# Loops written out on SyncE, TensorE and VectorE in a graph network's edge passes, and places freed eight at a time

## The chip, the cores and the metric

The kernel runs on one core of a Trainium2 chip. The core has a tensor engine (PE), a vector engine (DVE), a scalar engine (ACT), GpSimd (POOL), and SyncE (SP), which here only waits, counts and starts DMAs. Each engine works through its own program in order, and the engines meet at semaphores. The metric is the device time in microseconds (us) from the first to the last instruction; less is better.

## The reference

There are 12500 nodes with 128 features and 200000 edges, sorted by target. Two graph networks run one after the other.

```python
h = jnp.maximum(_layernorm(x, axis=-1), 0.0)
x = x + _L0_gnn_ref(h, src, dst, ...)          # two SAGE layers, each: segment_sum(h[src], dst) / degree, then a dense layer
h = jnp.maximum(_layernorm(x, axis=-1), 0.0)
x = x + _L1_gnn_ref(h, edge_index, edge_weight1, ...)   # two attention layers:
    # q, k, v = h @ Wq, h @ Wk, h @ Wv;  score = q[tgt] . (k[src] + e)
    # softmax of the scores over the edges of a target;  out = segment_sum(a * (v[src] + e), tgt)
    # gate with h @ Wskip, batch norm, relu, residual
```

## The kernel before, in words

The edges are cut into 1564 tiles of 128. A tile that crosses from one block of 128 target nodes into the next is visited once for each block, which makes 1664 steps. 32 steps are a chunk (52 chunks), two chunks are a pair (26 pairs), and 4 steps or 4 tiles are a group.

Four passes go over the edges: two aggregation passes (`sage_edges`, tags `first` and `second`) and two attention passes (`conv_edges`, one for each layer). Between them stand dense phases, and barriers part all phases.

**Aggregation pass.** POOL gathers one tile of source rows with each indirect DMA (L765) into a ring of 64 places, that is 16 groups. Before each group it waits until the semaphore `place_free` has come far enough (L761). ACT builds the one-hot matrices of the next chunk (`build`, L795 and L798) and releases the current step groups to PE one by one (`release`, L781 to L788), after it has read from small tables what tiles and PSUM banks the group needs. PE multiplies (L870), with the place and the bank of each step taken from registers that it loads from a table (L857). SP sits between PE and POOL: for each tile group it waits for the gathers (L718, which tells ACT through `tiles_in`), reads from the table `lastuse` which step group uses an older group of places last (L724 to L726), waits for that step group's sums (L727) and frees the places. The group freed is the one 8 groups back (`BEHIND`). DVE only moves finished banks out.

**Attention pass.** For each chunk DVE multiplies the gathered keys by PE's queries and sums them to scores (`multiply` L1478, `edge_term` L1493, `score_sum` L1483), runs a softmax that goes back and forth between DVE, PE and ACT (L1533 to L1586), weighs the values (L1506) and adds the 32 partial sums of PE (L1678) to the accumulators one after another (`add`, L1600 to L1606). The scores of the next chunk are worked in between. POOL gathers keys and values (L1457) and waits before each group for PE's sums of the chunk that used the places before. SP loads the small tables of the next chunk.

Chained instructions of one engine go through `Chain`: each counts a semaphore up, and `need` (L89) waits for a count. Inside a hardware loop (`Fori`, `chain.turns`) that count is a register, `self.base + mark`, so that the engine works it out first. The same holds for all waits and addresses that depend on the loop's number.

Of the kernel before, what the change touches and what calls it, by code (L numbers as in the profile page):

```python
# [41 lines left out]
KG = CH // GR  # L42
# [3 lines left out]
PAIRS = NC_ // 2  # L46
# [15 lines left out]
LAPS, REST = divmod(GROUPS, 2 * RG)  # L62
EARLY = 8
SUM_BANKS = 4
BEHIND = RG // 2
# [622 lines left out]
def sage_edges(nc, t, table, src_cols, tag, own, weight, bias):  # L688

    with room(nc, tag) as (sb, psum, sem):  # L690
# [16 lines left out]
        place_free, tiles_in, away_ready, sel_built, sel_ready, sums_ready, bank_free, chain_v = (  # L707
            sem(k) for k in ("place_free", "tiles_in", "away_ready", "sel_built", "sel_ready", "sums_ready", "bank_free", "chain_v"))

        with nc.Block() as block:  # L710
            @block.sync
            def _(sp):
# [7 lines left out]
                def half_lap(half, first):  # L720
                    for k in range(RG):
                        landed(k, half)
                        if k >= BEHIND or not first:
                            last = sp.value_load(lastuse[0:1, bass.ds(half * RG + (k - BEHIND), 1)],  # L724
                                                 min_val=0, max_val=STEPS // GR - 1)
                            sp.wait_ge(sums_ready, last + 1)  # L726
                            sp.sem_inc(place_free, 1)  # L727

# [18 lines left out]
                load_src(1, 3)  # L747
                with sp.Fori(1, LAPS - 1) as g:
                    for b in range(2):
                        half_lap(g * 2 + b, False)  # L750
                        load_src(b, g * 2 + (b + 2))
# [98 lines left out]
            def _(pe):  # L850
# [28 lines left out]
                pair(0)  # L879
                with pe.Fori(1, 2 * LAPS) as g:  # L880
                    pair(g)
# [459 lines left out]
KP = CH // PAIR  # L1341
# [8 lines left out]
def conv_edges(nc, t, tag):  # L1350

    with room(nc, tag) as (sb, psum, sem):
# [63 lines left out]
        with nc.Block() as block:  # L1416
            @block.sync
            def _(sp):
# [7 lines left out]

                with sp.Fori(0, PAIRS) as g:
                    for h in range(2):
# [33 lines left out]
            def _(dve):  # L1462
                chain = Chain(dve, chain_v)
# [172 lines left out]
                stages(chunk(0, 1), chunk(0, 0))  # L1636
                with chain.turns(PAIRS - 1, 2 * (2 * KG + 15 + KP)) as g:
                    stages(chunk(g + 1, 0), chunk(g, 1))
                    stages(chunk(g + 1, 1), chunk(g + 1, 0))
# [3 lines left out]
            def _(pe):  # L1643
# [78 lines left out]
                stages(chunk(0, 1), chunk(0, 0), chunk(1, 0))  # L1722
                with pe.Fori(0, PAIRS - 2) as g:
                    stages(chunk(g + 1, 0), chunk(g, 1), chunk(g + 1, 1))
                    stages(chunk(g + 1, 1), chunk(g + 1, 0), chunk(g + 2, 0))
# [457 lines left out]
```

## Time and profile before

| | us |
|---|---|
| median of 3 runs | 12163.2 |
| lowest, highest | 12148.79, 12170.95 |
| the profiled execution: its time | 12124.62 |
| its span, first to last instruction | 12122.7 |
| POOL busy | 6650.8 |
| PE busy | 5591.6 |
| ACT busy | 4685.4 |
| DVE busy | 3794.2 |

No engine is busy for much more than half of the span. The busy time leaves out everything that a sequencer does by itself: register work, branches, waits, DMA starts. The profile marks those with a q (SPq, DVEq), and it writes "issue" where an engine stood idle and waited for nothing that the profile shows, "remote" where the semaphore's source isn't in the record.

### The profile page before, as it was taken

The numbers are of one execution on the slowest core, as the hardware profiler recorded it, in microseconds if no ns is written. First come the engines' busy times: TensorE is split into PE (matmuls) and PEld (weight loads), VectorE is DVE, ScalarE is ACT, GpSimd is POOL, SyncE is SP. The second block draws the span as 40 slices with busy tenths as digits, with TensorE's granted clock in tenths as the row PEclk, the third lists the DMA queues.
The fourth block names the chain that finished last, engine by engine and source line by source line (L and its number), as shares of the span: only waits on it lengthen the run. The fifth ranks groups of instructions, "written<-read, shape, count | busy, mean of one in ns | idle before, by whom it ended". The sixth has DMA issues, their size and how long they took to land. (4 is left out here: it accounts for less than half of the span.)

```text
span 12122.7 us, 136052 instructions
## 1 busy us (share of the span) xinstructions
PE 5591.6 (46%) x23720; PEld 4740.3 (39%) x23721; DVE 3794.2 (31%) x11057; ACT 4685.4 (39%) x11029; POOL 6650.8 (55%) x6852
## 2 busy tenths in 40 slices
PE   0333333344443343454555555555645555555556
PEld 0333333333333333333444444444434444444444
DVE  3000000001000000034445554544744455545447
ACT  2333333333333333343444444444334444444443
POOL 4665555554565555555555555555445555555555
PEclk8555555566555555566666666666866666666667
DMA  5111111124111111134333333333243333333333
GB/s 102 50 52 49 49 50 49 49 65 128 49 51 50 48 48 49 48 104 124 113 112 112 111 113 110 111 114 113 79 131 112 111 112 109 115 111 111 113 113 88
DMA packets 623121, 1069.90 MB, mean 88 GB/s; under 512 B 213469, under 2 KB 396798, under 8 KB 622482
## 3 DMA queue, kind: packets, MB, share of 16 engines
q0 software_dynamic: 261920, 645.88, 19.2%
q1 hardware_dynamic: 281842, 368.09, 9.7%
q10 hardware_dynamic: 78848, 51.39, 1.5%
q14 instruction: 468, 3.83, 0.1%
q8 instruction: 43, 0.70, 0.0%
HBM read 961.58 MB, written 103.26 MB: 88 GB/s over the span
## 5 line engine op out<-in xcount | busy, mean ns | idle before, releaser
L1457 POOL DMA_INDIRECT conv_kv<-key_value,conv_src x3328 | 3287.0, 988 | 2925.8 <-PE conv_ps_sums L1678 1423.8
L1678 PE MATMUL conv_ps_sums<-conv_kv,conv_sel 128*128 128x136 f32 x6656 | 1509.3, 388 | 1428.2 <-DVE sums L1606 1124.7
L765 POOL DMA_INDIRECT second_msg<-sage_hidden_projected,second_src x1564 | 1477.1, 944 | 1135.3 <-SPq L727 534.2
L765 POOL DMA_INDIRECT first_msg<-sage_in,first_src x1564 | 1477.1, 944 | 1058.4 <-SPq L727 516.6
L1678 PEld LDWEIGHTS conv_ps_sums<-conv_kv,conv_sel 128*128 128x128 f32 x6656 | 1315.2, 280 | 1573.7 <-DVE sums L1606 1212.6
L1758 ACT ACTIVATE conv_selT<-conv_place,minus_partition 128x512 f32<-128x512 f32 x832 | 595.5, 716 | 3094.5 <-PE conv_ps_query L1664 1087.7
L1664 PE MATMUL conv_ps_query<-query_table,conv_selT 128*128 x6656 | 1585.8, 413 | 325.4 <-issue 277.2
L1664 PEld LDWEIGHTS conv_ps_query<-query_table,conv_selT 128*128 128x128 f32 x6656 | 1410.6, 308 | 420.6 <-issue 406.4
L870 PE MATMUL first_ps_sums<-first_msg,first_sel 128*128 x3328 | 832.0, 429 | 1524.4 <-ACTq L788 786.1
L870 PE MATMUL second_ps_sums<-second_msg,second_sel 128*128 x3328 | 832.7, 429 | 1473.6 <-ACTq L788 789.6
L1606 DVE TENSOR_TENSOR sums<-sums,conv_ps_sums 128x136 f32 x3328 | 972.5, 292 | 1506.2 <-remote 732.8
L870 PEld LDWEIGHTS first_ps_sums<-first_msg,first_sel 128*128 128x128 f32 x3328 | 718.5, 319 | 1651.1 <-issue 1651.1
L870 PEld LDWEIGHTS second_ps_sums<-second_msg,second_sel 128*128 128x128 f32 x3328 | 719.7, 319 | 1586.0 <-issue 1586.0
L1743 ACT ACTIVATE conv_sel<-iota_row,conv_rel 128x128 f32<-128x128 f32 x3328 | 1051.9, 386 | 59.7 <-PE conv_ps_sums L1678 59.1
L795 ACT ACTIVATE second_sel<-iota_row,second_rel 128x128 f32<-128x128 f32 x1664 | 556.9, 392 | 1185.0 <-issue 961.8
L795 ACT ACTIVATE first_sel<-iota_row,first_rel 128x128 f32<-128x128 f32 x1664 | 557.4, 392 | 1162.4 <-issue 922.6
L1478 DVE TENSOR_TENSOR conv_kv<-conv_ps_query,conv_kv 128x512 f32<-128x512 f32 x832 | 572.2, 688 | 1073.4 <-DMA after_hT<-conv_in_transposed 355.4
L834 DVE COPY sums<-second_ps_sums 128x129 f32 (+1 forms) x98 | 28.7, 293 | 2447.3 <-PE second_ps_sums L870 1112.0
L834 DVE COPY sums<-first_ps_sums 128x129 f32 (+1 forms) x98 | 28.7, 293 | 2426.5 <-PE first_ps_sums L870 1113.0
L1483 DVE TENSOR_REDUCE conv_score<-conv_kv 128x16 f32<-128x512 f32 x832 | 568.0, 683 | 0.0
L1763 ACT ACTIVATE conv_selT<-conv_selT 128x512 f32<-128x512 f32 x832 | 523.9, 630 | 61.9
L1746 ACT ACTIVATE conv_sel<-conv_sel 128x512 f32<-128x512 f32 x832 | 523.9, 630 | 26.3
(255 smaller groups left out, 5229.3 us busy)
## 6 DMA issues: line engine op xcount, KB each, us to landing
conv_place<-place_rows SPq DMA_DIRECT2D x416, 512.0 KB
conv_kv<-key_value,conv_src POOLq DMA_INDIRECT x3328
first_msg<-sage_in,first_src POOLq DMA_INDIRECT x1564
second_msg<-sage_hidden_projected,second_src POOLq DMA_INDIRECT x1564
conv_pen<-run_penalties SPq DMA_DIRECT2D x416, 48.5 KB
sage_own_hidden<-first_own_out ACTq DMA_DIRECT2D x49, 256.0 KB
sage_dense_own<-sage_own_hidden SPq DMA_DIRECT2D x14, 896.0 KB
sage_hidden_transposed<-sage_dense_hid SPq DMA_DIRECT2D x14, 896.0 KB
```

What stands on the lines that cost most here:

```text
L765: pool.indirect_dma_start(msg[:, j * MW:j * MW + D], None, table, bass.IndirectOffsetOnAxis(ap=src[:, b, j:j + 1], axis=0)).then_inc(gathe ...
L795: act.activation(sel[:, lo + i, :], t.iota[:, :], ACT.Abs, bias=rel[:, bass.ds(c * CH + (k * GR + i), 1)], scale=-1.0).then_inc(away_ready, 1)
L870: last = pe.matmul(ps[:, bass.ds(to[j] * 512, MW)], sel[:, h * CH + k * GR + i, :], msg[:, bass.ds(at[j] * MW, MW)], start=False, stop=Fal ...
L1457: pool.indirect_dma_start(kv[:, h * CH + j, :], None, t.kv_d, bass.IndirectOffsetOnAxis(ap=src[:, h, j:j + 1], axis=0)).then_inc(gathered[ ...
L1478: return mark(dve.tensor_tensor(keys, query(k)[:, :, :, 0:D], keys, ALU.mult))
L1483: return mark(dve.tensor_reduce(score[:, h, :, k * GR:k * GR + GR].rearrange("p h i -> p i h"), slots(h, k)[:, :, 0:D].rearrange("p i (h c ...
L1606: ins = dve.tensor_tensor(acc, acc, sums_of(h, step), ALU.add)
L1664: last = pe.matmul(psQ[:, 2 * (k % 2) + i // 2, (i % 2) * QW:(i % 2) * QW + QW], selT[:, k % SELG, P * i:P * i + P], t.qreg[:, bass.ds(at[ ...
L1678: last = pe.matmul(sums_of(h, step), sel[:, k % SELG, step % GR, :], kv[:, h * CH + step, DEN:2 * D], start=True, stop=True)
L1743: act.activation(sel[:, k % SELG, i, :], t.iota[:, :], ACT.Abs, bias=rel[:, h, j:j + 1], scale=-1.0).then_inc(away_ready, 1)
L1746: act.activation(sel[:, k % SELG, :, :], sel[:, k % SELG, :, :], ACT.Relu, bias=1.0, scale=-1.0).then_inc(sel_ready, 1)
L1758: act.activation(selT[:, k % SELG, :], place[:, q % 2, (k % 2) * GR * P:(k % 2 + 1) * GR * P], ACT.Abs, bias=t.minus[:, 0:1]).then_inc(awa ...
```

## The change

Loops that were hardware loops are now loops of the program's writer, so that each turn stands in the program with constants for its waits and addresses. This is done for SP and PE in all four edge passes, and for DVE in the two attention passes. ACT and POOL keep their loops, and so does DVE in the aggregation passes. Besides, SP frees the places of the aggregation ring for two groups at once, after the second of them.

```diff
                     for k in range(RG):
                         landed(k, half)
-                        if k >= BEHIND or not first:
+                        if k % 2 == 1 and (k >= BEHIND or not first):
                             last = sp.value_load(lastuse[0:1, bass.ds(half * RG + (k - BEHIND), 1)],
                                                  min_val=0, max_val=STEPS // GR - 1)
                             sp.wait_ge(sums_ready, last + 1)
-                            sp.sem_inc(place_free, 1)
+                            sp.sem_inc(place_free, 2)
...
-                with sp.Fori(1, LAPS - 1) as g:
+                for g in range(1, LAPS - 1):
...
-                with pe.Fori(1, 2 * LAPS) as g:
+                for g in range(1, 2 * LAPS):
...
-                with sp.Fori(0, PAIRS) as g:
+                for g in range(PAIRS):
...
-                with chain.turns(PAIRS - 1, 2 * (2 * KG + 15 + KP)) as g:
+                for g in range(PAIRS - 1):
...
-                with pe.Fori(0, PAIRS - 2) as g:
+                for g in range(PAIRS - 2):
```

```order
L1600 REGISTER_ALU
L1602 REGISTER_ALU [waits conv0_sums_ready]
L1606 ISA [waits conv0_ps_used]
L1606 TENSOR_TENSOR sums<-sums,conv_ps_sums 128x136
L89 REGISTER_ALU
L1606 ISA [waits first_gathered11]
L1606 TENSOR_TENSOR sums<-sums,conv_ps_sums 128x136
L95 REGISTER_ALU
L95 COMPARE_AND_BRANCH
L1533 TENSOR_TENSOR conv_score<-conv_score,conv_qwe 128x128 [waits first_gathered11,first_bank_free]
```

These are the same engine and place after the change.

```order
L1606 ISA [waits conv0_ps_used,conv0_sums_ready]
L1606 TENSOR_TENSOR sums<-sums,conv_ps_sums 128x136
L1606 ISA [waits first_gathered11]
L1606 TENSOR_TENSOR sums<-sums,conv_ps_sums 128x136
L1533 TENSOR_TENSOR conv_score<-conv_score,conv_qwe 128x128 [waits first_gathered11,first_bank_free]
```

Three of seven instructions of two adds are gone, and the branch with them. The address of the accumulator is still worked out (`ISA`), since it comes from a table.

The next rows are SP's in the first aggregation pass, before the change, for two tile groups.

```order
L724 ISA [waits first_sums_ready,first_gathered8]
L724 TENSOR_LOAD first_lastuse
L724 ISA x2
L726 REGISTER_ALU
L724 ISA [waits first_sums_ready,first_gathered9]
L724 TENSOR_LOAD first_lastuse
L724 ISA x2
L726 REGISTER_ALU
```

And these are SP's after the change, again for two tile groups.

```order
L724 TENSOR_LOAD first_lastuse [waits first_sums_ready,first_gathered8,first_gathered9]
L724 ISA x2
L726 REGISTER_ALU
```

One table read now serves two groups, and it comes after both have landed. On POOL nothing is moved: it asks for the places of one group at a time as before.

## Rows read from the trace of the kernel before

**Rows 1.** Stages of the program by engine; columns are in the first line.

```profile
core 0: us, PE busy (x) PEld busy (x) DVE busy (x) ACT busy (x) POOL busy (x), PEclk, DMA share, GB/s
215.00:2703.00 2488.00, 914.00 (x3625) 781.89 (x3626) 48.54 (x207) 877.72 (x2227) 1477.15 (x1564) 0.56 0.19 50
...
5500.00:8605.00 3105.00, 1588.53 (x7158) 1405.74 (x7159) 1542.89 (x4722) 1326.06 (x3017) 1641.43 (x1664) 0.63 0.37 111
```

**Rows 2.** Waits, 215 to 2703 us: who for whom, total us, times, longest.

```profile
ACT first_sel L795 <- issue: 922.6, 390, 15.0
PE first_ps_sums L870 <- ACTq L788: 786.1, 210, 26.1
POOL first_msg L765 <- SPq L727: 516.6, 142, 13.1
...
ACT first_sel L795 <- SPq L718: 74.1, 50, 6.3
```

**Rows 3.** SP's own waits in the same stretch.

```profile
SPq L727 <- PE first_ps_sums L870: 685.0, 180, 14.7
SPq L727 <- remote: 598.2, 95, 22.5
```

**Rows 4.** POOL's timeline from 1509 us: start, length, idle time before.

```profile
1511.18 0.94 POOL L765 DMA_INDIRECT first_msg<-sage_in,first_src  x1 [3.86 <-SPq L727]
1512.43 0.94 POOL L765 DMA_INDIRECT first_msg<-sage_in,first_src  x1 [0.30 <-issue]
...
1527.60 0.94 POOL L765 DMA_INDIRECT first_msg<-sage_in,first_src  x1 [1.74 <-SPq L727]
...
1540.37 0.94 POOL L765 DMA_INDIRECT first_msg<-sage_in,first_src  x1 [8.07 <-SPq L727]
...
1556.83 0.94 POOL L765 DMA_INDIRECT first_msg<-sage_in,first_src  x1 [1.77 <-SPq L727]
```

**Rows 5.** ACT's timeline around two releases, in the same columns.

```profile
1506.15 0.40 ACT L795 ACTIVATE first_sel<-iota_row,first_rel 128x128 f32<-128x128 f32 x1 [1.01 <-issue]
1507.54 0.40 ACT L795 ACTIVATE first_sel<-iota_row,first_rel 128x128 f32<-128x128 f32 x1 [0.99 <-issue]
...
1511.15 1.28 ACT L795 ACTIVATE first_sel<-iota_row,first_rel 128x128 f32<-128x128 f32 x4 [1.58 <-DVE first_ps_sums L835]
...
1514.09 1.28 ACT L795 ACTIVATE first_sel<-iota_row,first_rel 128x128 f32<-128x128 f32 x4 [1.00 <-SPq L718]
```

**Rows 6.** Register instructions of SP at L724: ns shortest/median/longest.

```profile
L724 SPq FUSED_REGOPS  x1392: 2/51/1408, 265.3 to 5279.5; - x199
```

**Rows 7.** Waits of the whole program: total us, times, longest.

```profile
POOL conv_kv L1457 <- PE conv_ps_sums L1678: 1423.8, 181, 32.3
DVE sums L1606 <- remote: 732.8, 150, 7.8
DVE sums L1606 <- issue: 398.9, 275, 5.3
DVE conv_score L1533 <- issue: 153.0, 48, 3.7
DVE sums L1606 <- PE conv_ps_sums L1678: 109.3, 94, 2.6
```

**Rows 8.** DVE's timeline over one pair of chunks in layer 1.

```profile
7071.45 0.35 DVE L1533 TENSOR_TENSOR conv_score<-conv_score,conv_qwe 128x128 f32<-128x128 f32 x1 [3.54 <-issue]
...
7117.17 0.30 DVE L1606 TENSOR_TENSOR sums<-sums,conv_ps_sums 128x136 f32 x1 [1.83 <-issue]
...
7126.97 0.28 DVE L1533 TENSOR_TENSOR conv_score<-conv_score,conv_qwe 128x128 f32<-128x128 f32 x1
...
7187.82 0.29 DVE L1533 TENSOR_TENSOR conv_score<-conv_score,conv_qwe 128x128 f32<-128x128 f32 x1 [3.08 <-issue]
```

**Rows 9.** POOL's timeline in the same pair, at two pauses.

```profile
7106.44 0.95 POOL L1457 DMA_INDIRECT conv_kv<-key_value,conv_src  x1 [3.09 <-PE conv_ps_sums L1678]
...
7124.38 0.95 POOL L1457 DMA_INDIRECT conv_kv<-key_value,conv_src  x1 [3.21 <-remote]
```

## The prediction

> **What bounds the kernel now.** I read the stages first [rows 1]. An aggregation pass takes 2488 us and an attention pass 3105; each has a twin of the same length within 1%, so the four make some 11190 of 12123 us. In neither kind is an engine busy for more than 60% of the time, so the bound is a chain of waits, and the change is in the code of exactly these stages.
>
> Then I read who waits for whom in the first aggregation pass [rows 2, 3]. A gather and the idle time behind it take 1.25 us (starts at 1511.18 and 1512.43 [rows 4]), so the 1564 gathers need 1955 us, and POOL alone isn't the bound. POOL stands 516.6 us for SP's L727 [rows 2], but SP itself stands at L727 for 685.0 + 598.2 us, 685.0 of it for PE's sums [rows 3]: SP passes on PE's lateness, it doesn't make it. PE in turn stands 786.1 us for ACT's release at L788, and ACT has 922.6 us of idle time with no releaser but its own issue [rows 2]. ACT waits only 74.1 us for SP's news of landed tiles. So the pass is held by ACT and PE, and ACT keeps its loop.
>
> What is ACT's "issue" time? Two instructions of one group start 1.39 us apart where they need 0.40 us (1506.15 and 1507.54), and soon after four of them take 1.28 us together, and two whole groups start 2.94 us apart (1511.15 and 1514.09) [rows 5]. SP's register instructions have a median of 51 ns and a longest of 1408 [rows 6]. So there are stretches in which an instruction takes some 0.7 us (half of 1.39, with one register instruction between two ACTIVATEs) instead of 0.05 on its sequencer. They lie late in POOL's unbroken runs of gathers: ACT was slow at 1506 to 1508, quick at 1511 to 1514 after POOL had paused for 3.86 us [rows 4, 5]. In the attention pass DVE's add at 7117.17 stands behind 1.83 us of "issue", late in the run of gathers that began at 7106.44 [rows 8, 9]. I call these the slow stretches. Work that becomes faster lets POOL go on without a pause, and that makes more of them; this feedback is what I expect to eat most of a gain.
>
> In the attention passes POOL stands 1423.8 us for PE's sums [rows 7], so there DVE and PE, with the chain between them, set the pace. DVE's own stalls at the adds are 398.9 us of "issue" (275 times) and 732.8 us "remote", and 153.0 us of "issue" (48 times, 3.2 us each) stand before L1533, the first instruction behind the loop's branch [rows 7].
>
> **The change part by part.** The sum is made against the profiled execution, 12124.6 us; the median of the runs, 12163.2, is 38.6 higher.
>
> SP written out in the aggregation passes: its program for two groups falls to under half. SP is waiting at L727 for half of the pass, and what waits for it in turn waits for PE. 0 us. If that cover were gone, it would be worth at most POOL's 516.6 us in this pass.
>
> PE written out there: one register instruction for a step group of 4, about 0.05 us, worked out ahead while PE waits for ACT. 0 us. The same in the attention passes, where PE waits for DVE.
>
> Places freed by eights: the first group of each pair is freed one PE group later. Nothing is queued behind POOL's wait but gathers. The cost has two ends. Low: 0, since POOL has 2488 - 1955 = 533 us to spare in a pass and fills a ring of 16 groups. High: of the four runs that [rows 4] begins, those at 1527.60 and 1556.83 are of a single group (their gathers end long before the next run). Such a run is over before a slow stretch begins; doubled, it lasts 10 us, and 5 of those may be slow. With a step group at 2.94 us when quick and about 9.7 us when slow (4 + 1 ACTIVATEs and 2 instructions of the release, times 1.39 us), 5 slow us lose 3.5 us. With at most 142 stalls in a pass [rows 2], a half of them before single groups, and half of these joined, that is 35 x 3.5 = 120 us a pass. I take 35 a pass, nearer to the low end, because POOL has its 533 us to spare, and a longer pause also gives back quick time: **+70 us** for both, bounds 0 and +240.
>
> DVE's branch: 153.0 us gross. But the pair shown tells what a pause is worth. From 7071.45 (after a pause of 3.54) to 7126.97 is 55.5 us; from 7126.97 (no pause) to 7187.82 is 60.9, of which 3.08 are the next pause, so 57.8 [rows 8]. The half without the pause before it needs 2.3 us more: two thirds of the pause are given back, as the softmax then meets a slow stretch. So a third of 153 is left: **-50 us**, bounds -153 and 0.
>
> [...]
>
> DVE's register work at the adds: 7 instructions for two adds become 4 (the listing above), and `multiply` loses two of its own. In quick stretches they run beside the previous add and cost nothing; only behind a real wait one of 0.09 us stands in the way, 94 + 150 times [rows 7]: **-20 us**. In slow stretches each counts. 3/7 of the 398.9 us of issue are 171 us. PE stands in the same slow stretch and must deliver the next sums, and POOL's pause of 3.09 or 3.21 us behind it [rows 9] shrinks by as much as DVE gains, so I take half: **-85 us**, bounds 0 and -171. If the "remote" stalls are of the same kind, 3/7 of 732.8 = 314 us more are to be had; I leave them out, since a semaphore that comes late isn't DVE's own instruction, and they extend the range.
>
> SP written out in the attention passes: it loads tables a chunk ahead, hidden behind 58 us of chunk. 0 us.
>
> Sum: +70 - 50 - 20 - 85 = -85 us, 12040 for the profiled execution, **12078** for the median.
>
> **The rivals.** (1) The forecast, a small gain: 12000 to 12135. Chance 0.38. (2) A large gain: the slow stretches become rarer because fewer instructions are issued, or the remote stalls shrink too. Then -153 - 171 - 314 = -640 at the far end, half of it 320: 11840. For it speaks that 1132 us of DVE's idle time stands before the adds; against it that ACT, with no change, has the same stalls, and that they follow POOL's runs. Chance 0.17. (3) Slower, by the eights: a run of one group becomes one of two. It decides when more than about 22 single runs in each pass are joined (22 x 3.5 x 2 = 154, against a gain of 155 at DVE). At its high end it gives +240 - 155 = +85 us or, if the gain at DVE is given back too, +240: 12250 to 12400; the likeliest is near the lower, 12270. For it: two of four runs shown are single. Against: POOL's 533 us to spare. Chance 0.29. (4) Nothing is left: the feedback takes back what DVE gains as it took two thirds of the branch's pause: 12163. Chance 0.16.
>
> **How the numbers follow.** About 0.2%, 24 us, is what a measurement of this kernel can tell from no change: the three runs lie 22 us apart. The time is that of (1), 12078. The range must hold 8 in 10: from 11840, the middle of (2), to 12280, just over the middle of (3); (1) alone is 12000 to 12135. Faster by over 0.2% are (1) but for its edge, and (2): 0.55. Same is (4) with little from (1) and (3): 0.17. Slower: 0.28.
>
> **What would show it.** In the profile after: the row "DVE conv_score L1533 <- issue" gone; attention passes some 75 us shorter each with "DVE sums L1606 <- issue" near 230; a pair's two halves alike, at 57 us or so. Aggregation passes 0 to 60 us longer, with fewer and longer stalls of POOL on SP, none shorter than a gather of eight apart, and ACT's issue time as it was. The prediction is wrong if an aggregation pass changes by over 120 us, which would mean that SP or PE was on its path, or if ACT's issue time falls, which would mean that the slow stretches depend on how many instructions the others issue. If the attention passes don't move although the branch's row is gone, the feedback is stronger than I took it.

## The result and the profile after

The changed kernel takes 11825.6 us (median of 4 runs, 11812.31 to 11838.88), the kernel before 12164.4 us beside it. The ratio is 0.9723 (95%: 0.9706 to 0.974), so the change gives 339 us. The forecast was 12078, a gain of 85, with a range from 11840; the result lies below that range. The profiled execution took 11830.03 us, its span is 11828.1, and the numbers below are from it.

These are the stages of the changed kernel that answer to [rows 1], an aggregation and an attention pass.

```profile
core 0: us, PE busy (x) PEld busy (x) DVE busy (x) ACT busy (x) POOL busy (x), PEclk, DMA share, GB/s
215.00:2728.00 2513.00, 906.44 (x3561) 774.53 (x3562) 44.76 (x197) 880.02 (x2227) 1475.33 (x1564) 0.55 0.19 50
5560.00:8492.00 2932.00, 1494.97 (x7160) 1342.26 (x7160) 1540.79 (x4722) 1320.44 (x3017) 1639.04 (x1664) 0.65 0.39 117
```

The attention pass is 173 us shorter (2932 against 3105). The next rows are DVE's adds of both attention passes, first in the kernel before and then in the changed one (ns shortest/median/longest, start of the first and of the last).

```profile
L1606 DVE TENSOR_TENSOR sums<-sums,conv_ps_sums x3328: 279/295/298, 5620.5 to 11945.8; 128x136 f32 x196
```

```profile
L1606 DVE TENSOR_TENSOR sums<-sums,conv_ps_sums x3328: 281/295/299, 5681.1 to 11653.5; 128x136 f32 x196
```

From the first to the last it is 6325 us before and 5972 after, 353 less. The first add comes 61 us later than before (5681.1 against 5620.5), so in these two executions the aggregation passes are longer by about that much. (One pair of executions says little here: in the kernel of the next section with DVE's attention loop alone, whose aggregation passes are those of before, the first add comes at 5672.9. The cost of the eights is read from the times below.) All of the gain is in the attention passes, and it is more than twice the 155 us that I forecast for them.

The waits of the whole program after the change answer to [rows 7] and, for ACT and POOL's L765, to [rows 2].

```profile
ACT first_sel L795 <- issue: 965.6, 397, 14.3
...
POOL conv_kv L1457 <- PE conv_ps_sums L1678: 908.3, 111, 32.3
...
POOL conv_kv L1457 <- remote: 627.2, 199, 3.3
...
POOL first_msg L765 <- SPq L727: 553.0, 103, 12.7
...
DVE sums L1606 <- issue: 243.2, 409, 3.8
...
DVE sums L1606 <- PE conv_ps_sums L1678: 128.1, 75, 3.1
...
DVE sums L1606 <- remote: 101.2, 64, 5.2
```

The kernel before has this row for POOL beside that of PE's sums:

```profile
POOL conv_kv L1457 <- remote: 457.4, 154, 3.4
```

The reader is to see four things. The row of L1533 behind the branch is gone. DVE's "issue" time at the adds fell from 398.9 to 243.2 us, as forecast (230). But the "remote" row, which I had left out of the sum, fell from 732.8 to 101.2: that is the largest move of all. And POOL stands 908.3 us for PE's sums where it stood 1423.8. A part of that only changed its name, since POOL's "remote" row rose from 457.4 to 627.2: the two together fell from 1881 to 1536 us, by 346, which is close to the 353 us that the attention passes gained. In aggregation ACT's issue time is as it was (922.6, now 965.6; in the three kernels of the next section that leave the aggregation passes alone it is 990.8, 942.1 and 985.6), and POOL has fewer stalls on SP that are longer (103 of 5.4 us each, before 142 of 3.6).

The timeline of DVE's L1533 after the change, one pair of chunks in the first attention pass, shows the two halves alike.

```profile
6823.36 0.28 DVE L1533 TENSOR_TENSOR conv_score<-conv_score,conv_qwe 128x128 f32<-128x128 f32 x1
...
6878.15 0.28 DVE L1533 TENSOR_TENSOR conv_score<-conv_score,conv_qwe 128x128 f32<-128x128 f32 x1
...
6934.21 0.28 DVE L1533 TENSOR_TENSOR conv_score<-conv_score,conv_qwe 128x128 f32<-128x128 f32 x1
```

That is 54.8 and 56.1 us. In [rows 8], which are from the same pass, the halves took 55.5 and 60.9.

### The profile page after: what moved, and what is told of

Same layout as the page of the kernel before. It is cut to its first block and busy times, and to the rows that moved or that the text cites. A ratio compares the mean times of both kernels' runs of the same rounds, so it can differ in the third digit from the quotient of the medians.

```text
span 11828.1 us, 120392 instructions
## 1 busy us (share of the span) xinstructions
PE 5386.2 (46%) x23720; PEld 4598.9 (39%) x23720; DVE 3790.0 (32%) x11057; ACT 4674.4 (40%) x11029; POOL 6635.3 (56%) x6852
## 5 line engine op out<-in xcount | busy, mean ns | idle before, releaser
L1457 POOL DMA_INDIRECT conv_kv<-key_value,conv_src x3328 | 3278.6, 985 | 2582.2 <-issue 927.6
L765 POOL DMA_INDIRECT second_msg<-sage_hidden_projected,second_src x1564 | 1475.2, 943 | 1160.3 <-SPq L727 548.4
L765 POOL DMA_INDIRECT first_msg<-sage_in,first_src x1564 | 1475.3, 943 | 1099.9 <-SPq L727 553.0
L1678 PE MATMUL conv_ps_sums<-conv_kv,conv_sel 128*128 128x136 f32 x6656 | 1442.3, 382 | 1096.1 <-DVE sums L1606 1018.9
L1664 PE MATMUL conv_ps_query<-query_table,conv_selT 128*128 x6656 | 1462.7, 388 | 287.9 <-issue 271.6
L1664 PEld LDWEIGHTS conv_ps_query<-query_table,conv_selT 128*128 128x128 f32 x6656 | 1296.9, 286 | 361.9 <-issue 338.3
L1606 DVE TENSOR_TENSOR sums<-sums,conv_ps_sums 128x136 f32 x3328 | 975.0, 293 | 784.9 <-issue 243.2
L1478 DVE TENSOR_TENSOR conv_kv<-conv_ps_query,conv_kv 128x512 f32<-128x512 f32 x832 | 569.4, 684 | 1663.5 <-remote 623.3
L795 ACT ACTIVATE first_sel<-iota_row,first_rel 128x128 f32<-128x128 f32 x1664 | 559.2, 392 | 1235.7 <-issue 965.6
L795 ACT ACTIVATE second_sel<-iota_row,second_rel 128x128 f32<-128x128 f32 x1664 | 556.9, 392 | 1211.2 <-issue 944.2
```

Of the source, the lines that this page charges most:

```text
L765: pool.indirect_dma_start(msg[:, j * MW:j * MW + D], None, table, bass.IndirectOffsetOnAxis(ap=src[:, b, j:j + 1], axis=0)).then_inc(gathe ...
L795: act.activation(sel[:, lo + i, :], t.iota[:, :], ACT.Abs, bias=rel[:, bass.ds(c * CH + (k * GR + i), 1)], scale=-1.0).then_inc(away_ready, 1)
L1457: pool.indirect_dma_start(kv[:, h * CH + j, :], None, t.kv_d, bass.IndirectOffsetOnAxis(ap=src[:, h, j:j + 1], axis=0)).then_inc(gathered[ ...
L1478: return mark(dve.tensor_tensor(keys, query(k)[:, :, :, 0:D], keys, ALU.mult))
L1606: ins = dve.tensor_tensor(acc, acc, sums_of(h, step), ALU.add)
L1664: last = pe.matmul(psQ[:, 2 * (k % 2) + i // 2, (i % 2) * QW:(i % 2) * QW + QW], selT[:, k % SELG, P * i:P * i + P], t.qreg[:, bass.ds(at[ ...
```

## The experiments

Runs on two groups of chips come up here, and they must be kept apart. On one group the kernel before takes 12164 to 12173 us; the profile shown ahead of the prediction, the result and the first eight experiments are from such chips. On the other group it takes 9099 to 9109 us. I call them the 12.2 ms chips and the 9.1 ms chips. The experiments on the first group are from two chips, those on the second from three. Each chip was used in one set of runs only, and the first group's came earlier, so the runs can't tell a property of the chip from a condition of the time. Each ratio is to the kernel before on the same chip.

**One part at a time, in the kernel before.** Four kernels, each the kernel before with one edit: DVE's attention loop, PE's, SP's, and the places by eights, in the order of this diff.

```diff
-                with chain.turns(PAIRS - 1, 2 * (2 * KG + 15 + KP)) as g:
+                for g in range(PAIRS - 1):
...
-                with pe.Fori(0, PAIRS - 2) as g:
+                for g in range(PAIRS - 2):
...
-                with sp.Fori(0, PAIRS) as g:
+                for g in range(PAIRS):
...
-                        if k >= BEHIND or not first:
+                        if k % 2 == 1 and (k >= BEHIND or not first):
...
-                            sp.sem_inc(place_free, 1)
+                            sp.sem_inc(place_free, 2)
```

Expected, DVE's attention loop:

> The kernel before with one edit: DVE's attention loop written out. In the changed kernel a chunk of the attention passes takes 55.0 us instead of 58.4, 3.4 x 104 = 355 us in all, and the aggregation passes are 57 us longer. Theory A (DVE's instructions were the cost: the branch comes back in full and its register work at the adds too, 'remote' stalls included): this kernel alone has nearly the whole of the 355, ratio 0.970 to 0.975, the 'remote' idle time of DVE at the adds falls from 733 us to under 200. Theory B (my forecast, the gain of DVE is half given back): ratio 0.987 to 0.992. Theory C (SP or PE written out in the attention passes carries a good part): ratio 0.980 to 0.990 with the remote stalls still above 400 us.

Expected, PE's attention loop:

> The kernel before with one edit: PE's attention loop written out. Theories A and B: PE's register work is hidden, ratio 0.998 to 1.001. Theory C (PE's sequencer is itself slow late in a run of gathers, so that its sums come late and POOL and DVE stand for it): ratio 0.985 to 0.995, and POOL's 1424 us behind PE's sums fall by over 100.

Expected, SP's attention loop:

> The kernel before with one edit: SP's attention loop written out. Theories A and B: SP loads tables a chunk ahead, so the ratio is 0.999 to 1.001. Theory C: SP's small loads come earlier and something of DVE's waits goes, ratio below 0.997.

Expected, places by eights:

> The kernel before with one edit: the places of the aggregation ring are freed for two groups at once, all loops kept. Theory A (the eights cost what the aggregation passes lost, 57 us): ratio 1.004 to 1.006. Theory D (the eights cost nothing or gain, and the 57 us are due to SP or PE written out there): ratio 0.997 to 1.001. My forecast had +70 us, ratio 1.006.

| edit alone | median us (before 12172.4) | ratio, 95% | us, from the ratio |
|---|---|---|---|
| DVE, attention | 11946.6 | 0.981 (0.9785 to 0.9835) | -231 |
| PE, attention | 12082.0 | 0.9928 (0.991 to 0.9946) | -88 |
| SP, attention | 12109.7 | 0.9949 (0.993 to 0.9968) | -62 |
| eights | 12227.3 | 1.0046 (1.0029 to 1.0063) | +56 |

Theories A and B fail, and theory C holds in its numbers: 0.981 for DVE, at the edge of its band, with a "remote" row that is still 447.3 us; 0.9928 for PE; 0.9949 for SP. PE and SP each give a part that I had put at nothing. For the eights it is theory A, 1.0046. The four sum to -325, and the change gave -337 by its ratio, so they add up.

The kernel with the eights alone has the attention passes of before, word for word, and so it tells how far the rows of these passes vary between two executions:

```profile
POOL conv_kv L1457 <- PE conv_ps_sums L1678: 1460.8, 209, 32.6
...
DVE sums L1606 <- remote: 692.9, 130, 8.5
...
DVE sums L1606 <- issue: 466.1, 296, 8.2
```

That is 37, 40 and 67 us off the rows of before, so a smaller move says nothing. POOL's two rows at L1457 vary less when they are taken together, and they follow the time of the attention passes, from the first to the last of DVE's adds in the same execution:

| profiled execution | POOL for PE's sums and "remote", us | first to last add, us |
|---|---|---|
| before | 1881 | 6325 |
| eights alone | 1894 | 6334 |
| DVE alone | 1656 | 6101 |
| PE alone | 1809 | 6264 |
| SP alone | 1820 | 6267 |
| changed | 1536 | 5972 |

So what each part brings is time that POOL no longer waits before its gathers.

Where PE's part comes from is in the waits of the kernel with only PE's loop written out.

```profile
POOL conv_kv L1457 <- PE conv_ps_sums L1678: 1208.9, 129, 32.4
...
POOL conv_kv L1457 <- remote: 600.1, 189, 3.4
...
DVE sums L1606 <- issue: 474.3, 322, 5.3
...
DVE sums L1606 <- remote: 272.2, 84, 6.2
```

DVE's program is untouched in it, and its own issue time is no less (474.3, before 398.9). What falls is "remote", from 732.8 to 272.2 [rows 7], and POOL's wait for PE's sums by 215, of which 143 come back in its own "remote" row. Only PE's program was changed, so most of the "remote" time at the adds was DVE's wait for sums that PE's loop had made late. The row is not the price: 461 us of it went, and the kernel gained 88. DVE now stands longer before L1478, its first instruction on gathered rows (its "remote" row there rose from 317.3 to 470.4 us, a row put down to a DMA from 355.4 to 461.6). With only DVE's loop written out the "remote" row at the adds falls too, to 447.3.

SP's part shows where SP loads the place rows for ACT (L1423 to L1424). First the register instructions of that line in the kernel before, then SP's wait at L1424 in the kernel before, and then the same wait with SP's loop written out. Durations are in ns, shortest/median/longest.

```profile
L1423 SPq ALU_OP  x312: 4/689/737, 5505.2 to 11865.8; - x156
```

```profile
SPq L1424 <- ACTq L1762: 357.9, 196, 7.2
```

```profile
SPq L1424 <- ACTq L1762: 1095.1, 182, 28.2
```

Half and more of SP's register instructions at this line took 0.69 us, and SP came so late that it waited for ACT only 358 us; written out it waits 1095 us, so it is now early. What it loads is not a chunk ahead: `place` has two buffers of a quarter chunk each. The median, though, is no measure of SP's lateness. The kernel with the eights alone has the same program for SP at this line, and its row is

```profile
L1423 SPq ALU_OP  x312: 4/33/737, 5569.4 to 11940.9; - x156
```

with a wait at L1424 of 308.4 us. With DVE's loop alone written out the median is 661, with PE's alone 33. In the four kernels 153 to 158 of the 312 take over 300 ns, so that the median tips from one side to the other; the longest, 737 in all four, tells that some do.

ACT turns these rows into `conv_selT`, from which PE makes the queries, and ACT's wait there is shorter as well, in the kernel before and with only SP's loop written out:

```profile
ACT conv_selT L1758 <- PE conv_ps_query L1664: 1087.7, 243, 11.7
```

```profile
ACT conv_selT L1758 <- PE conv_ps_query L1664: 881.0, 221, 8.0
```

The last step, from there to the 62 us, is argued and not shown. And there is another way, which the same kernel hints at: DVE's own issue time at the adds is the lowest of all kernels that keep the loops of DVE and PE.

```profile
DVE sums L1606 <- issue: 270.1, 243, 7.8
```

It is 398.9, 466.1 and 442.2 us in the three others (before, eights alone, `hint_back_edge=True`), and DVE's program is untouched in all but the last. So DVE's own stalls seem to depend on what SP issues. It is one profiled execution, and no run tells how the 62 us part between the two ways.

**The changed kernel with one part taken back, and the pause at the branch alone.** The first has `if k >= BEHIND or not first` and `sem_inc(place_free, 1)` again. The second keeps DVE's attention loop, the fourth the aggregation loops of SP and PE. The third is the kernel before in which DVE's loop stays, but is made with `hint_back_edge=True` (`hinted` is set for this loop alone):

```diff
-        with self.eng.Fori(0, count) as i:
+        with (self.eng.bass.Fori(0, count, engines=OrderedEngineSet([self.eng.engine]), hint_back_edge=True)
+              if hinted else self.eng.Fori(0, count)) as i:
...
-                with chain.turns(PAIRS - 1, 2 * (2 * KG + 15 + KP)) as g:
+                with chain.turns(PAIRS - 1, 2 * (2 * KG + 15 + KP), hinted=True) as g:
```

Expected, places by fours in the changed kernel:

> The changed kernel with the places freed one group at a time again. The eights alone cost 55 us in the kernel before (ratio 1.0046). Theory A (the parts add up): ratio 0.966 to 0.970 to the kernel before, the aggregation passes back to their old length. Theory B (with SP written out the eights save SP work it would otherwise be late with): ratio 0.971 or more.

Expected, DVE's attention loop kept in the changed kernel:

> The changed kernel with DVE's attention loop kept as a loop. DVE's loop alone gave 0.981 in the kernel before. Theory A (the parts add up): ratio 0.990 to 0.993. Theory B (DVE's work counts for more when PE and SP are quick, since nothing else holds the chunk): ratio 0.993 to 0.998. Theory C (PE and SP gained only what DVE would have gained anyway): ratio below 0.988.

Expected, `hint_back_edge=True` in the kernel before:

> [...] Theory A (the branch comes back in full, the rest of the 226 us of DVE's loop is register work): ratio 0.986 to 0.989. Theory B (my forecast, two thirds of each branch pause are given back): ratio 0.994 to 0.998. [...]

Expected, the aggregation loops of SP and PE kept in the changed kernel:

> The changed kernel with SP's and PE's loops of the aggregation passes kept as loops. Theory A (my forecast: SP and PE cost nothing there, ACT holds the pass): the ratio is that of the changed kernel, 0.971 to 0.975. Theory B (they gain there too, hidden beneath the cost of the eights): ratio 0.976 to 0.982. Theory C (written out they cost something, since more instructions are fetched beside the gathers): ratio under 0.970.

| kernel | median us (before 12173.1) | ratio, 95% |
|---|---|---|
| changed, by fours | 11776.1 | 0.9677 (0.966 to 0.9693) |
| changed, DVE's loop kept | 12051.7 | 0.9904 (0.9888 to 0.9921) |
| before, `hint_back_edge=True` | 12154.8 | 0.9989 (0.9979 to 0.9999) |
| changed, aggregation loops kept | 11843.1 | 0.9727 (0.9708 to 0.9747) |

Theory A holds in three of the four. The eights cost 0.0046 here too (0.9723 - 0.9677), 56 us. DVE's loop is worth 220 us (0.9904 - 0.9723) in the changed kernel and 231 in the kernel before. The aggregation loops of SP and PE are worth nothing that can be told (0.9727, 0.9708 to 0.9747, against 0.9723); some 20 us either way would not be seen. Written out they do bring more instructions in: from 300 to 2650 us the instruction queues of the profile moved 156 packets (1.56 MB) in the changed kernel and 117 (0.98 MB) in the one with these loops kept. The cost that theory C put on it isn't seen.

The third kernel has one more instruction of DVE's sequencer in each of the 50 turns; this is its row (ns shortest/median/longest, first and last start).

```profile
L96 DVEq BRANCH_PREFETCH_HINT  x50: 39/39/159, 5678.4 to 11845.8; - x50
```

The kernel tells what the pause before L1533 was worth, less what this instruction costs. Waits of that kernel, in which two more lines stand ahead, so that L1533 is L1535 and L1606 is L1608:

```profile
DVE sums L1608 <- remote: 692.8, 136, 9.2
DVE sums L1608 <- issue: 442.2, 275, 7.2
...
DVE conv_score L1535 <- issue: 31.6, 48, 1.3
```

The pauses fell from 153.0 to 31.6 us (3.2 to 0.66 us each, 48 times in both), and the time by 13 us (1 to 26). The other rows moved by 40 and 43 us in opposite directions, no more than they vary by themselves. So of 121 us taken away about a ninth came back; my forecast took a third of 153. Theory A, full return, is refuted, and even my range for theory B (0.994 to 0.998) was too generous. The rest of DVE's 231 us, some 218, isn't the pause behind the branch. It comes with register work that is less and, as the next rows show, quicker; the runs on 12.2 ms chips don't part the one from the other, nor either from the bare fact that the code is no longer a loop's.

How the register work is cheaper is seen in the instruction that stands in both kernels, the address of the accumulator. The first row is the kernel before, the second the kernel with only DVE's loop written out.

```profile
L1606 DVEq FUSED_REGOPS  x3224: 6/57/728, 5620.8 to 11945.7; - x190
```

```profile
L1606 DVEq FUSED_REGOPS  x3224: 57/57/57, 5673.2 to 11773.3; - x190
```

It is there 3224 times in both. Before, its longest is 728 ns; now none is over 57, and so it is in the changed kernel. My forecast took 3/7 of the stalls away, because three of seven instructions go, and left the other four as slow as they were. They weren't. Besides, two of the seven are the adds themselves: of five register instructions three go.

**Register work without the loop, and ACT's and POOL's loops.** The first kernel puts the turn's number into a register in straight code, and so keeps all register work but no branch:

```diff
-                with chain.turns(PAIRS - 1, 2 * (2 * KG + 15 + KP)) as g:
+                turn = dve.alloc_register(f"{tag}_turn")
+                start, per = chain.base + chain.n, 2 * (2 * KG + 15 + KP)
+                for u in range(PAIRS - 1):
+                    dve.reg_mov(turn, u)
+                    g = dve.snap(turn, min_val=0, max_val=PAIRS - 2)
+                    chain.base, chain.n = start + g * per, 0
...
+                chain.base, chain.n = start + (PAIRS - 1) * per, 0
```

> The kernel before with DVE's attention loop written out, but the turn's number is put into a register at the head of each turn, so that every wait and address is still worked out by the same register instructions. What is gone is the branch; what stays is the register work. Writing out with constants gave 0.981, and taking the branch's pause away alone 0.9989. Theory A (the register instructions are the cost, wherever they stand): ratio 0.997 to 1.000, and DVE's row 'ALU_OP' at L1602 still has a longest of 0.7 us and more. Theory B (it is the loop: code that is run a second time is delivered slowly, and straight code is not): ratio 0.980 to 0.985, with no DVE register instruction but the table reads over 0.3 us.

The second is the changed kernel with ACT's attention loop written out (`for g in range(PAIRS - 2)`):

> The changed kernel with ACT's attention loop written out too. Theory A (each engine's register work counts where it falls late in a run of gathers): ACT's register instructions in the attention passes show no long durations in the trace of before (unlike those of DVE and SP), so little is gained: ratio 0.970 to 0.973, against 0.9723 of the changed kernel. Theory B (it is enough that fewer instructions are issued by anyone): ratio 0.960 to 0.968.

The third is the changed kernel by fours with ACT's aggregation loop written out (`for g in range(1, 2 * LAPS - 1)`):

> The changed kernel with places freed one group at a time (0.9677) and ACT's aggregation loop written out. My reading is that ACT holds the aggregation passes, with 923 us of issue time before L795 in each, most of it register instructions at 0.7 us. About half of these instructions (the address of each ACTIVATE, the wait values) go, the table reads stay. If that reading is right: ratio 0.940 to 0.958, ACT's issue time falls from 953 to under 750 us, and each aggregation pass is 60 to 160 us shorter. If POOL or PE holds the pass: ratio 0.965 to 0.969.

The fourth is the third with ACT's attention loop, POOL's loops and DVE's aggregation loop written out as well:

> As the one with ACT's aggregation loop written out, and besides ACT's and POOL's loops in all edge passes and DVE's in the aggregation passes. If no engine's register work but ACT's in the aggregation counts further: within 0.3% of that kernel. If POOL's register work between groups delays gathers: up to 1% less. If the instructions now fetched for POOL in the aggregation and attention passes collide with its gathers: 0.3 to 1% more.

These ran on a 9.1 ms chip, and the changed kernel and all repeats on two more of them:

> The same kernel as the first with this name (DVE's attention loop written out with all register work kept). That one ran on a chip on which the kernel before takes 9109 us and no register instruction shows over 0.3 us, so it told nothing of the slow stretches. On a chip where the kernel before takes some 12170 us: theory A (the register instructions are the cost wherever they stand) ratio 0.997 to 1.000 and DVE's ALU_OP rows with a longest over 0.7 us; theory B (it is the code of a loop that is slow, straight code isn't) ratio 0.980 to 0.985. On the 9109 us chip: 0.9995 again.

> Again the changed kernel with places freed by fours and ACT's aggregation loop written out; 0.9985 on the 9109 us chip. On a chip where the kernel before takes some 12170 us: ratio 0.940 to 0.958 if ACT's register instructions hold the aggregation passes there, 0.965 to 0.969 if POOL or PE does.

> Again all loops of the edge passes written out on every engine, places freed by fours; 0.9982 on the 9109 us chip. On a chip where the kernel before takes some 12170 us: within 0.3% of the kernel with ACT's aggregation loop written out if no other engine's register work counts, up to 1% less if POOL's does.

> The changed kernel itself, beside the others of this call. On a chip where the kernel before takes some 12170 us: ratio 0.971 to 0.974 as measured. On the chip where it takes 9109 us: no slow register instruction there, and the changed kernel with ACT's attention loop written out besides gave 0.9981, so 0.997 to 1.000; the eights cost nothing there if their 57 us come from the slow stretches alone.

> The last two runs: the two questions that need a chip on which the kernel before takes some 12170 us. DVE's attention loop written out with all its register work kept. There: register instructions are the cost wherever they stand, ratio 0.997 to 1.000; the loop's code is what is slow, ratio 0.980 to 0.985. Where the kernel before takes 9105 to 9109 us: 1.000, and both questions stay open.

> The changed kernel with places freed by fours and ACT's aggregation loop written out. Where the kernel before takes some 12170 us: 0.940 to 0.958 if ACT's register instructions hold the aggregation passes, 0.965 to 0.969 if not. Where it takes 9105 to 9109 us: 0.9984 again.

| kernel | ratio in three sets of runs; before 9108.9, 9104.9, 9098.8 us |
|---|---|
| before, DVE flat with registers | 0.9995, 0.9998, 1.0001 |
| changed | -, 0.9986 (0.9976 to 0.9996), - |
| changed, ACT's attention loop out | 0.9981, -, - |
| changed by fours, ACT's aggregation loop out | 0.9985, 0.9984, 0.9986 |
| all loops of the edge passes out, by fours | 0.9982, 0.9984, - |

On a 9.1 ms chip the change is worth 13 us (0.9986 of 9105), a twenty-sixth of its worth on the other. None of the numbers that I expected on the 12.2 ms chips was tried there, so these runs tell nothing of ACT's part in that regime, nor whether register work in straight code would be slow. That more instructions brought in collide with the gathers doesn't show: with all loops out the instruction queues moved 635 packets (7.08 MB), with ACT's aggregation loop out 522 (6.14 MB), at ratios of 0.9982 and 0.9985. What the runs do show is where the difference sits. Two groups of instructions of the changed kernel on a 9.1 ms chip (count, then busy us and mean ns, then idle time before them by releaser):

```profile
L765 POOL DMA_INDIRECT first_msg<-sage_in,first_src x1564 | 1475.7, 944 | 530.8 <-issue 476.3 <-DMA first_src<-in_src_cols 54.5
...
L1606 DVE TENSOR_TENSOR sums<-sums,conv_ps_sums 128x136 f32 x3328 | 974.5, 293 | 521.9 <-DVE sums L1606 216.8 <-PE conv_ps_sums L1678 137.8 <-issue 5.8
```

POOL doesn't wait for SP at all in the aggregation (no row <-SPq), and DVE's "remote" time is gone. In the attention passes POOL's wait for PE's sums is 38.4 us. POOL's own stream is the bound of the aggregation there: 1564 gathers at 1.25 us are 1955 us, and the matmuls of the first pass run from 228.0 to 2155.4 us, 1927 us; before they took 2436 (261.3 to 2697.2) on the 12.2 ms chip. The next fence is POOL's timeline on the 9.1 ms chip, in the middle of an attention pass.

```profile
7108.92 0.95 POOL L1457 DMA_INDIRECT conv_kv<-key_value,conv_src  x1 [0.30 <-issue]
7110.17 0.95 POOL L1457 DMA_INDIRECT conv_kv<-key_value,conv_src  x1 [0.30 <-PE conv_ps_sums L1678]
7111.43 0.95 POOL L1457 DMA_INDIRECT conv_kv<-key_value,conv_src  x1 [0.30 <-issue]
```

And this is the same kernel on the 12.2 ms chip of the result.

```profile
7105.48 0.95 POOL L1457 DMA_INDIRECT conv_kv<-key_value,conv_src  x1 [0.30 <-issue]
7115.85 2.64 POOL L1457 DMA_INDIRECT conv_kv<-key_value,conv_src  x1 [9.42 <-PE conv_ps_sums L1678]
```

PE's sums are there in time on the one and 9.42 us late on the other. Gathers that follow each other without a wait start 1.25 us apart on both (7108.92 and 7110.17 on the 9.1 ms chip, 7104.23 and 7105.48 on the 12.2 ms chip).

## Why the prediction was wrong, point by point

**What bounds the kernel: right in what was tested.** With the aggregation loops of SP and PE kept or not, the time is the same, so my 0 us for both stands. The aggregation pass shown moved by 25 us (2488 to 2513), not by over 120, and ACT's issue time didn't fall. That ACT's loop holds the pass is not shown: written out, it was run on 9.1 ms chips alone.

**Eights, +70: right.** +56 us alone and +56 taken back. The mechanism was only seen in part. POOL's stalls are fewer and longer (142 to 103), as it wants. But the loss was to come from ACT in its slow stretches, and that isn't shown: ACT's issue time in both passes is 1884 us before, 1994 with the eights alone and 1910 in the changed kernel, and it is 1955 with only DVE's attention loop written out, which leaves these passes alone. That the size fits may be luck: it was picked near one end of 0 to 240.

**The branch, -50: mis-sized.** 13 us (1 to 26) for 121 of the 153 us. I had read from a single pair [rows 8] that two thirds of a pause are given back; it was nine tenths. A pause of 3.2 us sits behind the branch, 48 times in the kernel before; what it comes from, no run here shows. Writing the loop out does pay here, but the pause accounts for 13 of DVE's 231 us.

**DVE's register work, -20 and -85: the wrong size from a wrong assumption.** What DVE's loop cost beside the pause was some 218 us, 113 more than the 105 of the forecast. The step "3/7 of the 398.9 us of issue" counted instructions that go, with the two adds among the seven; the ones that stay became quick too (728 ns longest to 57). And I left the "remote" stalls out, 285 us of which (732.8 to 447.3) went with DVE's loop alone. No run shows the -20 us for quick stretches by itself, nor its 0.09 us for one instruction: the medians in the trace of before are 40 ns at L89, L1600 and L1602 and 57 at L1606.

**SP and PE in the attention passes, 0: the step that failed.** "0 us. The same in the attention passes, where PE waits for DVE." and "SP written out in the attention passes: it loads tables a chunk ahead, hidden behind 58 us of chunk. 0 us." were -88 and -62 us, 150 of the 254 us by which the forecast missed. DVE's 113 are the next largest part. PE's loop and SP's both had a row in the trace of before that I read wrongly or didn't read. For PE it was "DVE sums L1606 <- remote: 732.8, 150, 7.8" in [rows 7]. I wrote that a semaphore that comes late isn't DVE's own instruction, which is so, and stopped there instead of asking whose it is. The sum it waits for is PE's, as the run with PE's loop alone showed, and I had put PE's loop at nothing because PE waits for DVE; but PE waited 1124.7 us for DVE's adds, as this row of the kernel before says, and DVE for most of its 732.8 for PE. Waits in both directions are a chain through both, in which either one's lateness can count.

```profile
PE conv_ps_sums L1678 <- DVE sums L1606: 1124.7, 415, 7.8
```

For SP it was the row of L1423, with half of its register instructions at 0.69 us. I had read L724 alone, of the aggregation, and the two buffers of `place` stand in the code. How SP's earlier loads become 62 us stays open.

**The rivals.** Rival (2), the large gain, was the case, at its middle (11840, measured 11825.6), and I had given it 0.17. That the number fits is luck in part: "half of the far end" was no mechanism, and its terms were DVE's instructions alone, where PE's and SP's brought 150 us. Of its two ways, slow stretches that become rarer or remote stalls that shrink, the second is shown. The first is not excluded: ACT's issue time did not fall, but DVE's did, from 398.9 to 270.1 us, with only SP's loop written out. Against this rival I had held that ACT has the same stalls with no change; that says nothing of DVE, PE and SP. Rival (3) needed a gain at DVE of 155 or less. Rival (4), full feedback, nearly holds for the branch's pause and not for register work.

**What stays open.** What a slow register instruction comes from. These rows show that neither "code in a loop" nor "register work beside gathers" is the whole rule. The first is SP's L724 after the change, in straight code on a 12.2 ms chip.

```profile
L724 SPq FUSED_REGOPS  x376: 3/147/730, 273.9 to 5324.0; - x188
```

The second is the same line of the same kernel on a 9.1 ms chip.

```profile
L724 SPq FUSED_REGOPS  x376: 147/147/187, 250.7 to 4196.6; - x188
```

The third is ACT's L1745 in the attention passes of the kernel before, on a 12.2 ms chip, inside a loop and beside gathers.

```profile
L1745 ACTq ALU_OP  x672: 35/35/35, 5656.8 to 11796.1; - x168
```

Straight code can be slow (730 ns at the longest), and loop code can be quick (35). Whether DVE's register work would be quick in straight code on a 12.2 ms chip, and what ACT's loops cost in aggregation there, was run three times, and only on 9.1 ms chips. Nor do the runs show what makes a chip one or the other, or whether it is the chip.

The best version found is the changed kernel with places freed by fours: 11776 us, 0.9677 (0.966 to 0.9693), on a 12.2 ms chip. On a 9.1 ms chip that version with ACT's aggregation loop written out (0.9985) and the changed kernel (0.9986) are alike.

## What to carry to other kernels

When two engines wait for each other in a chain, price the instructions of both: neither could be taken as hidden by the other's wait here (PE's loop was worth 88 us, where PE waited 1124.7 us for DVE). A row "remote" can be somebody's lateness (461 of 732.8 us went with PE's loop); find whose semaphore it is before leaving it out of the sum. Before calling a fall of it a gain, look where the wait went: here the sum of POOL's waits before its gathers followed the time, and the single rows did not. Read the shortest, median and longest duration of the register instructions at every line that the change touches, on each engine: a longest of 700 ns where the shortest is a few ns (4/689/737 at L1423, in a loop that was worth 62 us) hints at a cost that no table of busy time shows, and the median can fall on either side of it (33 to 689 at the same line). And a gain of this sort may belong to the chip (339 us on one, 13 on another): measure on more than one before trading code size for it.

## What the runs showed of the hardware

The kernel before takes 12164 to 12173 us on some chips and 9099 to 9109 on others, a quarter less, with gathers at 1.25 us each on both. For the changed kernel the mean granted clock is 0.626 on the one and 0.673 on the other. The clock can be a small part of the difference at most: PE is busy for 5386.2 and 5166.8 us, 219 apart, where the spans are 2733 apart. The longest register instructions tell the two apart. Of the changed kernel's 30 groups of a hundred or more register instructions (by line, engine and op) 11 have a longest of over 300 ns on the one, from 702 to 1422; none has on the other, where the longest of all is 248. In the kernel before on a 12.2 ms chip 25 of 52 groups do, in the kernel with DVE's loop flat on a 9.1 ms chip none of 50. This is SP's L1423 on a 9.1 ms chip, in the kernel with DVE's loop flat, where SP's program is that of the kernel before; the 12.2 ms chip had 4/689/737.

```profile
L1423 SPq ALU_OP  x312: 32/33/33, 4422.7 to 8845.8; - x156
```

ACT's L795 shows it in the aggregation of the changed kernel. First the 12.2 ms chip, with the idle time before the line by its releasers:

```profile
L795 ACTq FUSED_REGOPS  x2816: 2/46/1414, 389.8 to 5163.2; - x188
...
  issue: 1909.8, 801
  remote: 160.2, 48
  SPq L718: 89.6, 47
```

and then the 9.1 ms chip:

```profile
L795 ACTq FUSED_REGOPS  x2816: 37/46/51, 289.8 to 4013.2; - x188
...
  SPq L718: 1570.0, 328
  issue: 132.3, 52
```

On the one ACT stands for itself, on the other for the gathers that SP reports, which is POOL's stream. The whole change is worth 339 us on the first and 13 on the second.
